# A first pass over the edges that adds its rows into a table in SBUF, instead of writing running sums to memory

## The reference

```
agg_sum  = segment_sum(x[src], dst)                    # per node: sum of the rows of its sources
agg_mean = agg_sum / max(count, 1)
h        = concat([x, agg_mean]) @ W0                  # = x @ W0x + agg_mean @ W0a
x        = layernorm(x + h)
```

## Time and profile before

| | us |
|---|---|
| median of 3 runs | 5207.69 (5198.79 to 5208.72) |
| the profiled execution's own time | 5200.82 |
| its span in the trace | 5198.9 |
| L0, its span in the trace | about 0 to 1069 |
| N0 | about 1069 to 1197 |
| mean granted PE clock | 0.681 |

### The profile page before, as it was taken

How to read it: one execution, slowest core, us unless ns; L and a number is a source line. 1 busy time by engine, 2 the same in 40 slices (tenths; PEclk the granted TensorE clock), 3 DMA queues, 4 the chain that set the end, 5 groups by cost and what they waited for, 6 DMA issues and landing times. The chain is left out here.

```text
span 5198.9 us, 82680 instructions
## 1 busy us (share of the span) xinstructions
PE 3451.3 (66%) x19084; PEld 2648.9 (51%) x19084; DVE 3446.6 (66%) x6723; ACT 1663.5 (32%) x3857; POOL 3879.2 (75%) x4265
## 2 busy tenths in 40 slices
PE   4444444356666666664888888877764787888784
PEld 3333333343444444443666666656653566666662
DVE  6555322235888888873777777779886566666665
ACT  1111111133333333342222222248873122222225
POOL 7777777767777777767777777769877777777773
PEclk7555555568888888885555555569997677777776
DMA  7555555524555555534666666659994677777762
GB/s 227 174 167 175 160 167 175 166 80 149 167 172 169 172 169 171 167 104 136 175 174 174 174 174 173 174 164 316 309 297 141 207 213 217 212 217 215 215 209 70
DMA packets 785645, 946.92 MB, mean 182 GB/s; under 512 B 216039, under 2 KB 500977, under 8 KB 785524
## 3 DMA queue, kind: packets, MB, share of 16 engines
q1 hardware_dynamic: 435604, 397.84, 25.7%
q0 software_dynamic: 144320, 323.10, 23.1%
q10 hardware_dynamic: 205600, 224.71, 12.6%
HBM read 583.78 MB, written 361.50 MB: 182 GB/s over the span
## 5 line engine op out<-in xcount | busy, mean ns | idle before, releaser
L521 POOL DMA_INDIRECT L_gath<-in_x,src x832 | 787.8, 947 | 266.9 <-issue 231.6
L521 POOL DMA_INDIRECT L_gath<-tab,src x832 | 793.0, 953 | 256.4 <-issue 244.7
L521 POOL DMA_INDIRECT L2a_gath<-tab_h,src x832 | 788.2, 947 | 253.7 <-issue 251.2
L521 POOL DMA_INDIRECT L_gath<-tab_kv,src x832 | 787.2, 946 | 253.5 <-issue 221.8
L657 ACT ACTIVATE L_back<-L_pB 128x512 f32<-128x512 f32 x624 | 365.5, 586 | 959.2 <-PE L_pB L627 899.3
L639 DVE TENSOR_TENSOR_SCAN L_acc<-L_mask,L_acc,L_pT 128x512 f32<-128x512 uint8 x207 | 264.7, 1279 | 544.2 <-PE L_pT L585 544.1
L585 PE MATMUL L_pT<-ident,L_gath 128*128 128x128 f32 x832 | 224.4, 423 | 537.9 <-DMA L_gath<-in_x,src 535.9
L627 PE MATMUL L_pB<-ident,L_acc 128*128 128x128 f32 x2496 | 511.2, 344 | 0.8 <-DVE L_acc L778 0.5
L627 PEld LDWEIGHTS L_pB<-ident,L_acc 128*128 128x128 f32 x2496 | 401.8, 181 | 154.9 <-issue 148.5
L585 PEld LDWEIGHTS L_pT<-ident,L_gath 128*128 128x128 f32 x832 | 145.0, 212 | 614.5 <-DMA L_gath<-in_x,src 485.6
L875 PE MATMUL L_pM<-L_hid,w_W 128*128 128x512 f32 x416 | 293.2, 794 | 184.0 <-DVE L_acc L913 182.4
(11 more groups left out here) (293 smaller groups left out, 7738.0 us busy)
## 6 DMA issues: line engine op xcount, KB each, us to landing
run<-L_back ACTq DMA_DIRECT2D x416, 256.0 KB, 3.0
L_seed<-seed SPq DMA_DIRECT2D x416, 256.0 KB, 3.5
run<-L_back ACTq DMA_DIRECT2D x208, 264.0 KB
seed<-L_zeros SPq DMA_DIRECT2D x52, 1024.0 KB
sent<-L2a_gath ACTq DMA_DIRECT2D x208, 256.0 KB, 2.9
L_sent<-sent SPq DMA_DIRECT2D x208, 256.0 KB, 4.3
run<-L_back SPq DMA_DIRECT2D x208, 256.0 KB, 4.6
L_mask<-same SPq DMA_DIRECT2D x104, 256.0 KB, 3.7
```

Source lines behind the costliest of these rows:

```text
L521: gp.indirect_dma_start(out=gath[k][:, t, :], out_offset=None, in_=table, in_offset=bass.IndirectOffsetOnAxis(ap=g["src"][:, tile:tile + 1 ...
```

## The change

- A new class `Ranks` numbers the distinct targets. From two copies of `dst` laid out as 104 rows of 1024 (8 tiles a row) DVE marks where a target begins, scans the marks, and with a triangular matmul gets each row's offset. It yields, for each edge, its target's rank counted from the head of the edge's tile (`local`), for each tile an offset from its batch's base (`tile_off`), and for each batch a base (`batch_base`); the last two go to DRAM and come back as one line in one partition.
- In L0 `turn`, the scan, `ret`, ACT's copy and the store of `run` are gone, and so are the mask's loads. Instead DVE makes `pick`, four 128 x 128 one-hot marks a batch; PE clears a bank with a matmul of zeros and adds, tile by tile, `gath^T @ pick` at the columns given by `tile_off`, read into a register with `value_load` (three per batch); DVE reads the batch's base with `value_load` and adds the 512 columns into `sums`, a table [128, 6784] in SBUF. SP's loop holds only the fills.
- `vector_after` and `tensor_after` also give each node tile's first rank (`node_base`) and each node's place among the ranks of its tile (`place`, spread over all partitions through DRAM).
- In N0 nothing is fetched. `prep` reads a base per node tile with `value_load` (four per batch), copies 128 columns of `sums` to `win`, and makes marks `agg` from `place`; PE multiplies `win` by `W0a` (instead of turning), ACT copies as before, and `result` spreads the rows to the nodes with `agg` as weights; `gather_up` multiplies by `mean` tile by tile.

```diff
+            def into_ranks(n, k, r):
+                need(pe, s_pick, n)
+                room(pe, s_add, n, 2)
+                pe.matmul(pW[k % 2][:, :], beside.nought[:, :], nought_row, start=True, stop=False, skip_group_check=True)
                 landed(pe, s_gath, k, r, BT)
-                room(pe, s_scan, n, 2)
                 for t in range(BT):
-                    m = pe.transpose(pT[k % 2][:, cols(t)], gath[k][:, t, :], g["ident"][:, :])
+                    at = pe.value_load(ranks.tile_off[0:1, bass.ds(n * BT + t, 1)], min_val=0, max_val=BE - P) if t else 0
+                    m = pe.matmul(pW[k % 2][:, bass.ds(at, P)], gath[k][:, t, :], pick[k % SLOTS][:, t, :], start=False, stop=t == BT - 1, skip_group_check=True)
                 m.then_inc(s_turn, 1)
-            pipeline(pe, half, DEEP, [(0, turn), (1, beside.tensor_stage(pe)), (2, ret)])
+            pe.wait_ge(ranks.s_line, 32)
+            pipeline(pe, half, DEEP, [(0, into_ranks), (1, beside.tensor_stage(pe))])
...
+            def marks(n, k, r):
+                room(v, s_turn, n, SLOTS)
+                v.tensor_tensor(pick[k % SLOTS][:, :, :], row.unsqueeze(1).to_broadcast([P, BT, P]),
+                                ranks.local[:, bass.ds(n * BT, BT)].unsqueeze(2).to_broadcast([P, BT, P]), ALU.is_equal).then_inc(s_pick, 1)
+
+            def add(n, k, r):
+                at = v.value_load(ranks.batch_base[0:1, bass.ds(n, 1)], min_val=0, max_val=NP - 1)
+                need(v, s_turn, n)
+                room(v, s_add, n, 1)
+                here = sums[:, bass.ds(at, BE)]
+                v.tensor_tensor(here, here, pW[k % 2][:, :], ALU.add).then_inc(s_add, 1)
+            ranks.vector_first(v, pR, pW[0])
             setup.vector_first(v)
+            v.memset(sums[:, :], 0.0).then_inc(s_zero, 1)
-            pipeline(v, half, DEEP, [(0, beside.vector_stage(v)), (0, scan)])
+            pipeline(v, half, DEEP, [(0, marks), (0, beside.vector_stage(v)), (1, add)])
...
-            pipeline(act, BATCHES, SLOTS, [(2, copy_rows(act, back, pB, s_ret, s_back, s_out)), (2, store_rows(act, run, back, s_back, s_out))])
-            all_stored(act, s_out)
...
-            load, fill = group_load(sp, g["same8"], mask, s_mask, s_scan, s_mgo), beside.sync_stage(sp)
-            pipeline(sp, BATCHES, DEEP, [(0, load), (0, fill)])
+            pipeline(sp, BATCHES, DEEP, [(0, beside.sync_stage(sp))])
+            beside.sync_after(sp)
...
-        fetch_rows(gp, index, table, got, s_got, s_go)
+        if layer:
+            fetch_rows(gp, index, table, got, s_got, s_go)
...
             if layer == 0:
-                v.tensor_tensor(sums, mine, over(g["mean"][:, span(n)], m), ALU.mult).then_inc(s_agg, 1)
+                room(v, s_turn, n, NSLOTS)
+                for t in range(m):
+                    at = v.value_load(g["node_base"][0:1, n * BT + t:n * BT + t + 1], min_val=0, max_val=NP - 1)
+                    ins = v.tensor_copy(win[k][:, t, :], g["sums"][:, bass.ds(at, P)])
+                ins.then_inc(s_win, 1)
+                room(v, s_y, n, NSLOTS)
+                v.tensor_scalar(rows(agg[k][:, 0:m, :]), g["place"][:, flat(n)], g["lane1"][:, 0:1], None, ALU.is_equal).then_inc(s_agg, 1)
...
+                        ins = v.scalar_tensor_tensor(y[k][:, t, :], pY[:, cols(t)], g["mean"][:, tile:tile + 1], g["x"][:, tile, :], ALU.mult, ALU.add)
```

More of the change, by code:

```diff
@@ L202, in build @@
             g["xT"] = early.enter_context(nc.sbuf_tensor("xT_early", [P, NT * P], F32))
-            edges_sum(nc, d, g)
-            nodes(nc, g, 0, out)
+            with ExitStack() as first:
+                for name, shape, dtype in (("sums", [P, RANKS], F32), ("node_base", [1, NT], I32), ("place", [P, NP], U8), ("lane1", [P, 1], F32)):
+                    g[name] = first.enter_context(nc.sbuf_tensor("f_" + name, shape, dtype))
+                edges_sum(nc, d, g)
+                nodes(nc, g, 0, out)
             edges_max(nc, d, g)
@@ L543, in edges_sum @@
         gath, s_gath, s_go = edge_buffers(ph, D)
[L544 to L549, removed]
-        s_mask, s_out = ph.slot_sems("mask", 2), ph.slot_sems("out", SLOTS)
-        run = g["run"].rearrange("(p t) f -> p t f", p=P)
-        pX = [ph.ps("pX"), pT[1]]
-        setup, beside = Setup(ph, d, g), NodeEdges(ph, d, g)
+        pick = [ph.sb(f"pick{k}", [P, BT, P]) for k in range(SLOTS)]
+        pW = [ph.ps(f"pW{k}") for k in range(2)]
+        pR = [ph.ps(f"pR{k}") for k in range(2)]
+        s_turn, s_pick, s_add, s_zero = (ph.sem(n) for n in ("turn", "pick", "add", "cleared"))
+        pX = [ph.ps("pX"), pW[1]]
+        setup, beside, ranks = Setup(ph, d, g), NodeEdges(ph, d, g), Ranks(ph, d, g)
         half = beside.STEPS
-        s_own, s_added, s_mgo = ph.sem("own"), ph.sem("added"), ph.sem("mgo")
+        s_own, s_added = ph.sem("own"), ph.sem("added")
+        sums = g["sums"]
         turns = [half + j * 2 * DEEP for j in range(5)] + [BATCHES]
@@ L611, in _ @@
                     v.tensor_tensor(mine, pX[0][:, 0:m * P].rearrange("p (t f) -> p t f", t=m), mine, ALU.add).then_inc(s_added, 1)
-                pipeline(v, end, DEEP, [(0, scan)], first=first)
+                pipeline(v, end, DEEP, [(0, marks), (1, add)], first=first)
         @block.scalar
@@ L629, in turn_back @@
     return ret
-def running_sum(v, pT, mask, acc, s_turn, s_mask, s_ret, s_scan):
-    def scan(n, k, r):
-        need(v, s_turn, n)
-        landed(v, s_mask, k // SLOTS, r)
-        room(v, s_ret, n, SLOTS)
-        room(v, s_scan, n, 1)
-        v.tensor_tensor_scan(acc[k % SLOTS][:, :], mask[k // SLOTS][:, in_group(k)], pT[k % 2][:, :], start_of(acc, n, k), ALU.mult,
-                             ALU.add).then_inc(s_scan, 1)
-    return scan
 def store_rows(eng, run, back, s_back, s_out):
@@ L1593, in _, with rank_rows @@
     def _(pe):
+        def rank_rows(n, k, r):
+            need(pe, s_win, n)
+            room(pe, s_aT, n, 1)
+            for t in range(count(n)):
+                m = pe.matmul(pA[:, cols(t)], win[k][:, t, :], w["W0a"][:, :], start=True, stop=True)
+            m.then_inc(s_turn, 1)
         def turn_agg(n, k, r):
@@ L1609, in result @@
                 need(pe, s_aT, n)
+                need(pe, s_agg, n)
                 for t in range(count(n)):
[L1611 removed]
+                    m = pe.matmul(pY[:, cols(t)], agg[k][:, t, :], aT[k][:, cols(t)], start=True, stop=True)
             else:
@@ L1638, in root_rows @@
             m.then_inc(s_root, 1)
-        steps(NB, NSLOTS, {0: [(0, turn_agg), (4, turn_new), (1, result), (5, tables)],
+        steps(NB, NSLOTS, {0: [(0, rank_rows), (4, turn_new), (1, result), (5, tables)],
                            1: [(5, tables), (0, turn_agg), (4, turn_new), (0, hidden), (1, result)],
```

132 lines of the change are left out of this document (116 added, 16 removed).

## The result

| | before | after |
|---|---|---|
| median of four runs, us | 5207.07 (5198.79 to 5208.72) | 5242.11 (5224.73 to 5253.06) |
| ratio, 95% interval | | 1.0067 [1.0048, 1.0086] |
| the profiled execution, its span | 5200.82, 5198.9 | 5224.73, 5223.0 |
| L0: POOL's last gather ends | 1056.99 | 1101.64 |
| N0's first instruction | 1069.02 | 1110.17 |

The forecast was 5186, faster by 17 us. The kernel became slower by 0.67%, 35 us. The profiled execution is the shortest of its four runs, and its span is only 24 us longer than before's. From L1 on both kernels run the same code, so the account ends at L1's first gather, where the changed kernel is 31.65 us late; behind it this one execution was 7.6 us quicker.

A forecast was written before the change was run, and what follows sets the result against it. POOL's gathers were taken to bound L0, and POOL alone N0 from 1131 us on. L0 +0.1 and N0 -17.3 gave -17.2, 5183.6 against the profiled 5200.82, written as 5186; range 5165 to 5240.

The forecast's parts named there:

- The load, L: Register load from SBUF on PE and DVE: taken as 0.4 us, between 0.057 and 2.3.
- The formula for PE's period: PE's time per batch in L0's first half: 0.43 + 0.48 + 3 max(L, 0.48) + 0.52 = 2.9 us.
- Rival 1: Slow loads between PE's products in L0 and on DVE in N0: at 1.35 us, +118, 5319; chance 0.22.
- rival 3: Full DMA queues from unspaced fills in L0: +21 to the middle, about +4 in sum, 5205; chance 0.05.
- its case of L = 1.0: Slow loads of 1.0 us: +12 at the start, +2 middle and end, +12 in N0, 5227.
- It hides if L is below 0.48: PE in L0: a load runs while the product before it computes (0.48 us), so shorter loads cost nothing.
- Start: L0's start: rank arithmetic and clearing, 11 to 15 us, hide in DVE's 20.1 us wait; first turn +1.3.
- Middle: POOL's 9.45 us wait in L0's middle grows by 2.1 of added chain and a longer turn, +3.4.
- End: L0's tail from last landing to N0: 8.44 us becomes 3.85, -4.6.
- N0: Fetches gone: first `comb` after 30 us, then 76.2, last scatter 1.3; 107.5 instead of 124.8, -17.3.
- The port pair: N0: DVE's SBUF copies lock GpSimd out of writing descriptors, so the sum would rise by 1 to 2 us.
- three signs of being wrong: PE idle inside a batch above 0.7 us a tile; DVE's start-up past 48 us; N0's `comb` over 7.5 us apart.

The follow-up runs named there:

- e1: The changed kernel with the zero fills again spaced by DVE's progress, one each 20 us; 5207.4 us, ratio to before 1.0013.
- e4: e1 with PE's three register loads a batch issued ahead of the batch's waits; 5201.4 us, ratio to before 1.0000.
- e5: The kernel before with 48 of its 52 fills in a burst at the front, the last four behind all mask loads; 5214.2 us, ratio 1.0012.
- e2: The changed kernel without PE's register loads, products at fixed columns (sums not the reference's), fills unspaced; 5194.5 us, ratio to before 0.9988.
- e12: e11 with the marks of batches 104 and 105 made ahead of the 30 small VectorE operations; 5186.7 us, ratio to before 0.9972.
- e6: e4 with the x @ W0x products spread, one batch of nodes to a stretch instead of three; 5197.6 us, ratio to before 0.9981.
- e8: e4 with N0 reading fixed columns, without DVE's four loads per batch (sums of other nodes); 5192.8 us, ratio to before 0.9971.
- e7: e4 with N0's order turned, a batch's first stage last on PE, DVE and ACT; 5201.2 us, ratio to before 0.9988.
- e9: The kernel before with only the x @ W0x products spread, one batch of nodes to a stretch; 5186.8 us, ratio 0.9983.
- e11: e4 with both the spread products of e6 and the N0 order of e7; 5185.9 us, ratio to before 0.9972.
- e10: e11 with the rank scan's inputs loaded first and most of the table cleared ahead of the scan; 5185.4 us, ratio to before 0.9976.

## Why the prediction was wrong

- **The load, L: the step that failed.** I took one value, 0.4 us, for all of L0. With quiet queues it was near: 0.30, and 0.15 for the register operation behind it. While the fills run it is 0.96 and 0.15, that is 1.1. The formula for PE's period came close at both: with 1.1 it gives 0.43 + 0.48 + 3 x 1.1 + 0.52 = 4.7, and 4.67 was measured; with the quiet value it gives 2.9, and e1 had 2.6. The sentence "52 MB ... some 240 us in which the DMA engines are full" and the sentence on L stood in one text and were never put together. Rival 1 asked what a slow load costs, rival 3 what full queues cost, and what happened is rival 3 causing rival 1, close to its case of L = 1.0 (5227). The place was right too, batch 32. From the changed kernel's own rows, PE begins at 52.6 and POOL would issue that gather at 181.8, so the bound is 4.17 a turn, and 31 turns at 4.67 are 15.6 us late: the stall of 16.1. In all it was +22 where the forecast had 0. Why full queues slow the load stays open. (In before that gather starts at 173.07, one ahead of the row that I took at 174.32, so the bound was 4.02.)
- **"It hides if L is below 0.48"** held only while PE had batches waiting. Where PE waits for a landing, each load adds 0.45 (e4), and that is what the end and part of the middle missed.
- **Full queues alone** were overpriced at up to 21 us (e5: 6 us). Landings did not reach 10 us (e2: 6.5 at most).
- **Start**, +1.3 forecast, +6.8 measured. The rank arithmetic was sized well, the clearing too (5.71 us, forecast 4 to 8). What was left out is the order: the rank work stands first on DVE and its inputs land at 22.4 us, so the masks of `Setup`, 11 us that DVE did from 13.2 us on before, now run from 31.0 to 42.0. DVE's 20 us of idle time before its first scan went into that as well as into the new work. PE's own turning of `x` ended 2 us later as well.
- **Middle**, +3.4 forecast, +5.7 measured, and another 8 from three later stalls of 3 us. I added operations to the chain. Of the 15.11 us the loads are 1.9 (e4). The larger matter is that PE now needs DVE before it can turn (e12), and that a slower batch no longer absorbs a round of three products (e6).
- **End**, -4.6 forecast, -3.5 measured: the products take 3.42, not 1.92, the loads again. With them early the end gives 4.5 (e12: 7.5 us against 12.0).
- **N0**, -17.3 forecast, -9.5 measured. The fill is 35.8 us, not 30: loads (e8: 12 us less) and the order on PE, where the first product of a new batch waits for DVE's next step ahead of finished work (e7: 3 us less). I had written that this product "fills PE's idle time"; in an order that can't be passed it holds up what stands behind it. The last scatter ends 7.1 us behind the last `comb`, not 1.3, since the last batches' `comb`s come closer than four scatters take (5.15 us). Between the first and the last `comb` 3.6 us came back instead, 72.4 where before has 76.0 (the prediction wrote 76.2).
- **The port pair.** The rule of "SBUF — State Buffer" in the Trainium skill, by which I allowed 1 to 2 us, is not borne out here: N0's scatters last 982 ns in both kernels (median of 49; the longest 1031 and 1028) and land in 2.3, with DVE's copies from `sums` beside them in one only.

Two of the prediction's three signs of being wrong came up in the first trace: PE's idle time inside a batch is above 0.7 us (0.79 and 0.85), and DVE's start-up ends after 48 (first marks at 51.72). The third did not: N0's `comb`s come 6.0 us apart.

The mechanism behind the gain was right, and most of its size: in e12, with loads early, fills spaced and marks ahead, from the end of the last gather (1057.94) to L1's first (1180.49) are 122.6 us against 140.1 before, -17.5 where the forecast had -21.9. But the fairest comparison is with e9, which is 0.17% below before without any of the change. Against its ratio the best kernels here are 0.0007 to 0.0011 ahead, within the intervals; and timed on the same chip as e9 (5186.8), e11 and e10 have medians of 5185.9 and 5185.4. So no gain of the change over e9 is shown. In the traces L1 starts 6.3 us sooner in e12: the end of L0 and N0 give 18.0 us against e9, and stalls at the start (9.29 us) and in the middle, which e9 does not have, take 11.7 back.

## What to carry to other kernels

Before a wait is removed, ask what it paced on its queue: here a mask's load had spaced 52 MB of fills, and their price fell on an instruction that seemed to have nothing to do with DMA. Price a dependent register load for the traffic that will run beside it, and let it hide only where the engine has work queued; where the engine waits, its whole length on the sequencer counts, so issue it ahead of the wait. And when work moves to another engine, list whom the bound engine now needs before it can release: a stall that an independent transpose would have bridged comes back when the product needs marks from a busy VectorE.

## What the runs showed of the hardware

- A register load from SBUF on PE's sequencer: 299 ns median in quiet time (294 to 307), 958 to 976 with the DMA engines' share near 1; on DVE's 303 ns in N0, and 957 to 982 in L0 while the queues are full. Before each copy that uses one DVE is idle for 0.51 us. The table of measured facts in "DMA: Bandwidth & Descriptors" of the Trainium skill has about 600 ns as the floor; the trace has half of it when the queues are quiet, and more than it when they are full. Why full queues slow it is open: no run measured the load's path.
- A product of fp32 matmuls (two records) costs PE 0.48 to 0.52 us a tile in a row of four (1.92 to 2.07), and 1.63 from start to start with a slow load between (189.96 to 191.59), at a granted clock of 0.50.
- Full queues delay a gather's landing by 2 to 4 us: 4.6 to 6.5 us from a batch's last issue to PE's first product in e2, 2.5 when the fills are out. In the kernel before a burst of 48 fills of 1 MB cost about 6 us (e5).
